# A gated delta rule with its slots refilled: four banks for the output transposes, first gathers first, no zero products, and two of four gate products in slots 10 and 11

## Chip, core and metric

The kernel runs on one core of one Trainium2 chip. The metric is device time in microseconds (us) of one execution. Engines are named as in the profile: PE (TensorE matmuls), PEld (its weight loads), DVE (VectorE), ACT (ScalarE), POOL (GpSimd), SP (SyncE).

## The reference, cut to what matters

Two layers, post-normed, on x of 16 sequences of 512 tokens with 256 channels, all in float32: gated linear attention, a mixture of 8 experts (top 2), the gated delta rule, and an MLP whose weights are composed from 32 of 64 primitives.

```python
x = _layernorm(x + _L0_attn_ref(x, ...))       # gated linear attention
x = _layernorm(x + _L0_ffn_ref(x, ...))        # mixture of experts
x = _layernorm(x + _L1_attn_ref(x, ...))       # gated delta rule, below
x = _layernorm(x + _L1_ffn_ref(x, ...))        # MLP with composed weights
# _L1_attn_ref: H = 4 heads, keys of 64, values of 128
h = rmsnorm(layernorm(x)); q, k, v = silu(causal_conv4(h @ Wq / Wk / Wv)); q, k = l2norm(q), l2norm(k)
g = -exp(A_log) * softplus(h @ Wa + dt_bias); beta = sigmoid(h @ Wb)
S = S * exp(g_t); S = S + k_t (x) ((v_t - k_t S) * beta_t); o_t = q_t S           # over 512 tokens
o = rmsnorm(o) * silu(h @ Wg); x = x + o @ Wo; out = gelu(layernorm(x) @ W2 + b2) + x
```

## The kernel before

The program is a sequence of stages, each with a queue written by hand for every engine and semaphores between them: `linear_attention`, `route` (router's top 2, slot tables and, beside them, the composed weights), `experts_mlp`, `delta_rule`, `mlp`. Engines meet in a barrier between stages.

`route` sums 16 pairs of weight tiles (`compose1`, `compose2`) into four PSUM banks `acc`. `edge(first)` (L248 on) multiplies a tile of zeros into all four banks, to open the sums with `start=True` and again to close them. It is called four times; `acc_done` behind the closing ones lets ScalarE copy the banks out.

`delta_rule` handles one sequence b (512 tokens, four chunks of 128) as a pipeline over periods. In period b four things run at once, told apart by flags: `ln`, the combination of expert outputs and the norms of sequence b+2; `front`, projections, convolutions and transposes to tokens of b+1; `here`, the inversion and the first two chunks of b; `past`, the last two chunks, gate, output norm, output projection and the dense layer of b-1; `end`, the last sum and norm of b-2. A loop runs the periods in pairs; the first and last ones stand outside it.

A period has 16 slots, two passes (pairs of chunks) of eight. In every engine's queue the order inside a slot is written out in its `period` function:

- PE. Slot n below 8: `project(n)`, with `to_tokens(n-2)` before it. `chunk(t, part)` in the slots of `CHUNK_AT`. Slots 0 and 8: `key_products`. Slots 5 to 7 and 13 to 15: three levels of the inversion (`first_half`, `second_half`), each of two tiles, which share the bank `UT` for T's transposes and have a bank each, `YZ[0]` and `YZ[1]`, for products. Slots 1 to 4: `gate(0..3)`, the products h @ Wg of b-1, all four through the bank `SIDE`. Slots 9 to 11: the four transposes `turn_o` of the gated output, through `SIDE` as well, each waiting for the copy of the one before (`turned_o` on ACT). Slots 11, 12: `mix_out`, o @ Wo, through `SIDE`.
- ACT. Slots 1 to 4: SiLU of the gate products. Slot 5: `squares(3)` and `squares_qk`, ahead of slot 6's copies `half_level`. Slot 8: `unit_o`, 16 scalings of the output, with one signal (`og`) at its end. Slots 9 to 11: `turned_o` and `rates`; slot 12: `rates(1)`, `channels(0)`.
- DVE. `products` turns the key products into nAT and QD, tile by tile; `conv(n-1)` in slot n; `last_sum(b-2)` and `last_norm(b-2)` in slots 9 and 10; `norm2(b+2)` in 10; `residual` in 11 and 12.
- SP and POOL. After `products` (semaphore `qd`) SP sends the 16x16 diagonal blocks of nAT to DRAM and gathers them for POOL, which inverts them (`invert_blocks`, 30 small instructions), and SP returns them into T (`return_blocks`). `first_half` of the lowest level (slots 5 and 13) waits for their landing (`t_in`). POOL also computes the powers -1/2 for all norms, gathers the expert rows (`gather_rows`, eight indirect DMAs a sequence) and, at the start of the stage, makes the constants (`ready`) before the first gather.

`mlp` (the last stage) copies the first block of its input behind the last (`tail_in`) and waits for that copy before it loads its weights.

## Time and profile before

| | |
|---|---|
| median of 3 runs | 4717.77 us (4705.86 to 4723.58) |
| profiled execution, its own time | 4709.05 us |
| its span, first to last instruction | 4707.4 us |
| granted TensorE clock, mean | 0.907 |
| busy: PE, PEld, DVE, ACT, POOL | 86%, 67%, 53%, 42%, 22% |
| instructions | 72598 |

The profile names each instruction by its line and tiles and says what ended the idle time before it. The granted clock is 1 at 2.4 GHz and 0.5 at 1.2 GHz; a mean over a stretch tells how much of it was at which level. A matmul of float32 shows as several records.

### The profile page before, as it was taken

The page shows a single profiled execution, that of the slowest core. Times are in us where ns is not written, and L with a number is a line of the kernel's source. Part 1 is how long each engine was busy: PE and PEld are TensorE (multiplying, and loading weights), DVE is VectorE, ACT ScalarE, POOL GpSimd, SP SyncE. Part 2 cuts the span into 40 slices and gives each one's busy share as a digit, 9 for nine tenths or more (in the row PEclk, how much of TensorE's full clock was granted, in tenths as well). Part 3 has the DMA queues.
Part 4 walks back from the last instruction along what each step waited for, and adds up shares of the span by engine and source line. Part 5 has one row for each costly group of instructions (what it writes and reads, how often), then busy time and mean ns, then how long its engine had stood idle before and what let it go on. Part 6 is the DMA issues. An engine that isn't in the chain of part 4 may idle for free. (4 is left out here: it accounts for less than half of the span.)

```text
span 4707.4 us, 72598 instructions
## 1 busy us (share of the span) xinstructions
PE 4038.7 (86%) x23892; PEld 3132.2 (67%) x23892; DVE 2471.9 (53%) x5457; ACT 1984.9 (42%) x4069; POOL 1055.9 (22%) x1689
## 2 busy tenths in 40 slices
PE   5887887689999999966888888888888888859998
PEld 3555555368888888854666667666666666646666
DVE  7888887432222222225666676766666766421111
ACT  5656564112112211214565565555555555422222
POOL 0111111101221122123333333333333332200000
PEclk8888888899999999987899898888898988879999
DMA  1100100344555555541111111111111110011111
GB/s 33 37 32 27 41 28 28 102 139 171 179 181 189 185 179 181 190 131 52 37 37 37 42 37 41 41 41 32 40 33 37 41 40 21 22 37 58 58 57 46
DMA packets 220431, 345.98 MB, mean 73 GB/s; under 512 B 99956, under 2 KB 171380, under 8 KB 201972
## 3 DMA queue, kind: packets, MB, share of 16 engines
q1 hardware_dynamic: 196404, 271.69, 18.2%
q0 software_dynamic: 23760, 71.07, 4.8%
q8 instruction: 126, 2.06, 0.2%
q14 instruction: 141, 1.16, 0.1%
HBM read 275.56 MB, written 67.63 MB: 73 GB/s over the span
## 5 line engine op out<-in xcount | busy, mean ns | idle before, releaser
L539 ACT ACTIVATE moe_rel<-moe_fc 128x512 f32<-128x512 f32 x284 | 169.6, 597 | 798.7 <-PE moe_fc L504 798.7
L504 PE MATMUL moe_fc<-moe_xT,moe_win 128*128 128x256 f32 x2272 | 504.0, 380 | 1.5 <-issue 0.8
L515 PE MATMUL moe_o<-moe_wout,moe_hT 128*128 128x256 f32 x2272 | 502.0, 379 | 0.0
L504 PEld LDWEIGHTS moe_fc<-moe_xT,moe_win 128*128 128x128 f32 x2272 | 432.9, 191 | 61.2 <-issue 2.1
L515 PEld LDWEIGHTS moe_o<-moe_wout,moe_hT 128*128 128x128 f32 x2272 | 426.3, 190 | 55.1
L563 DVE TENSOR_TENSOR moe_hT<-moe_rel 128x512 f32<-128x512 f32 x284 | 196.6, 692 | 366.5 <-ACT moe_rel L539 366.5
L1781 DVE SCALAR_TENSOR_TENSOR gdr_y<-gdr_bank,gdr_cw,gdr_y 128x511 f32<-128x511 f32 (+2 forms) x384 | 287.5, 749 | 52.6 <-ACT gdr_y L2045 29.0
L2242 PE MATMUL gdr_bank<-gdr_hT,gdr_wqkv 128*128 128x512 f32 x512 | 282.5, 680 | 21.3 <-ACT gdr_qk L2060 15.8
L572 DVE COPY moe_osb<-moe_o 128x512 f32<-128x512 f32 x71 | 49.1, 692 | 424.9 <-PE moe_o L515 424.9
L2361 PE MATMUL gdr_bank<-gdr_ident,gdr_T 128*128 128x128 f32 x768 | 132.5, 301 | 126.5 <-DMA gdr_T<-blocks_in 76.0
L693 PE MATMUL ffn_fc<-ffn_xT,ffn_win 128*128 128x512 f32 x512 | 224.0, 596 | 2.0 <-DMA ffn_win<-ffn_w 2.0
L704 PE MATMUL ffn_o<-ffn_wout,ffn_hT 128*128 128x256 f32 x1024 | 225.2, 381 | 0.0
L737 DVE TENSOR_TENSOR ffn_z<-ffn_o,ffn_xres 128x512 f32<-128x512 f32 x32 | 20.6, 686 | 384.3 <-PE ffn_o L704 384.3
L2365 PE MATMUL gdr_bank<-gdr_T,gdr_nAT 128*128 128x64 f32 x1536 | 215.6, 289 | 0.0
L718 ACT ACTIVATE ffn_hT<-ffn_fc 128x512 f32<-128x512 f32 x128 | 76.4, 597 | 328.2 <-PE ffn_fc L693 328.2
L2361 PEld LDWEIGHTS gdr_bank<-gdr_ident,gdr_T 128*128 128x128 f32 x768 | 102.6, 157 | 166.8 <-issue 74.6
L704 PEld LDWEIGHTS ffn_o<-ffn_wout,ffn_hT 128*128 128x128 f32 x1024 | 193.2, 190 | 27.6
L2365 PEld LDWEIGHTS gdr_bank<-gdr_T,gdr_nAT 128*128 128x128 f32 x1536 | 211.6, 213 | 0.0
L1673 POOL TENSOR_TENSOR gdr_rstd<-gdr_var,gdr_mhalf 128x4 f32<-128x4 f32 x64 | 65.1, 1017 | 648.7 <-DVE gdr_var L91 500.7
L2142 ACT COPY gdr_U<-gdr_bank 128x512 f32<-128x512 f32 x192 | 112.4, 585 | 215.2 <-PE gdr_bank L2361 206.1
L2242 PEld LDWEIGHTS gdr_bank<-gdr_hT,gdr_wqkv 128*128 128x128 f32 x512 | 100.3, 212 | 138.3 <-issue 84.0
L693 PEld LDWEIGHTS ffn_fc<-ffn_xT,ffn_win 128*128 128x128 f32 x512 | 97.8, 191 | 118.9 <-issue 118.2
(394 smaller groups left out, 8591.8 us busy)
## 6 DMA issues: line engine op xcount, KB each, us to landing
moe_win<-in_moe_w SPq DMA_DIRECT2D x71, 1024.0 KB, 8.0
moe_wout<-in_moe_w SPq DMA_DIRECT2D x71, 1024.0 KB, 5.1
slots_out<-moe_osb POOLq DMA_DIRECT2D x71, 256.0 KB, 7.4
ffn_xin<-mixed_rows SPq DMA_DIRECT2D x17, 512.0 KB, 3.8
gla_xp<-in_xT_rows SPq DMA_DIRECT2D x16, 512.0 KB, 4.7
gla_xres<-in_x_rows SPq DMA_DIRECT2D x16, 512.0 KB, 3.9
token_rows<-gla_x POOLq DMA_DIRECT2D x16, 512.0 KB, 3.4
rt_W<-in_fc_b SPq DMA_DIRECT2D x32, 256.0 KB, 3.3
```

The costliest lines, as they stand in the source:

```text
L504: ins = nc.tensor.matmul(fc_ps[j][:, m % 2, :], win[u][:, c, m * P:(m + 1) * P], xT[:, c, :], start=(c == 0), stop=(c == DT - 1))
L515: ins = nc.tensor.matmul(o_ps[u][:, t, :], hT[u][:, k, t * P:(t + 1) * P], wout[u][:, k, :], start=(k == 0), stop=(k == FT - 1))
L539: nc.scalar.activation(rel[:, j, :, :], fc_ps[j][:], ACT.Relu).then_inc(relu_done, 1)
L563: nc.vector.tensor_tensor(hT[u][:, 2 * j:2 * j + 2, :], rel[:, j, :, :], rel[:, j, :, :], ALU.mult).then_inc(h_ready, 1)
L693: ins = nc.tensor.matmul(fc_ps[m % 4][:], win[:, c, m * P:(m + 1) * P], xT[:, c, :], start=(c == 0), stop=(c == DT - 1))
L704: ins = nc.tensor.matmul(o_ps[t // 2][:, t % 2, :], hT[:, k, t * P:(t + 1) * P], wout[:, k, :], start=(k == 0), stop=(k == FT - 1))
L718: nc.scalar.activation(hT[:, m, :], fc_ps[m % 4][:], ACT.Gelu_apprx_tanh).then_inc(h_ready, 1)
L1781: ins = stt(y[:, n % 4, d:L], bank[FRONT[n % 2]][:, 0:L - d], cw[:, n, 3 - d:4 - d], y[:, n % 4, d:L], ALU.mult, ALU.add)
L2142: done("U", n, copy(U[t][:], heads(bank[UT][:])))
L2242: ins = mm(bank[FRONT[n % 2]][:], wqkv[:, c, n * P:(n + 1) * P], hT[:, c, :], start=(c == 0), stop=(c == DT - 1))
L2361: ins = tp(bank[UT][:, h * P:(h + 1) * P], T[:, i, h, :], ident[:])
L2365: ins = mm(bank[YZ[i]][:, h * HP:(h + 1) * HP].rearrange("p (m n) -> p m n", n=half), nAT[:, i, h, :], first, start=True, stop=True)
```

## The change

It changes which slot holds what, and the banks; the computation is the same. In words:

1. `route`: the products with zeros are gone. The first real product opens each sum and the last closes it; ScalarE waits for `used` in place of `acc_done`.
2. `mlp`: the tail copy is issued behind the weights, and waited for there.
3. Delta rule, start: the first input load is SP's first transfer; the gathers of sequence 0 are POOL's first work, the gathers of sequence 1 follow in its period -2, and the constants come behind them. PE, DVE and ACT wait for `ready` at the start of period -1 and not of the stage; DVE scales the weights in slot 5 of period -2.
4. `products`: all nAT of a pair first, with a semaphore `na` of their own that SP's `send_blocks` waits for, then all QD.
5. `gate(2)` and `gate(3)` of b-1 stay, now in slots 1 and 2; `gate(0)` and `gate(1)` of sequence b itself are made in slots 10 and 11 of period b, in the banks `YZ`, with their SiLUs in ACT's slot 12. PE waits for those (and for the second residual) before slot 13's first half.
6. `turn_o(0..3)` in slot 9, one bank each (`UT`, `YZ[0]`, `YZ[1]`, `SIDE`), each waiting only for its head's scaling; `unit_o` by heads in slots 7 and 8; `mix_out(0)` at the start of slot 10 in `SIDE`, `mix_out(1)` in slot 11 in `UT`.
7. ACT: `squares(3)` and `squares_qk` in slot 6 behind the level's copies, `decay_keys(2)` and `(3)` in slot 11, `lengths_u` in slot 12. PE: `rates` ahead of `to_tokens(7)` in slot 9. DVE: `last_sum` in slot 2, `last_norm` in 4, `lengths` in 7, `rates` in 9 and 10, `residual` in 10 and 11, `norm2` in 11, `rms` in 13 and 14. POOL: the power for `last_norm` ahead of the others.

```diff
@@ route @@
-                def edge(first):
-                    for bank in acc:
-                        ins = mm(bank[:], zero[:, 0:P], zero[:], start=first, stop=not first, skip_group_check=True)
-                    return ins
-                                 start=False, stop=False, skip_group_check=True)
+                                 start=(k == 0), stop=(k == KT - 1), skip_group_check=True)
-                    act.wait_ge(acc_done, n + 1)
+                    act.wait_ge(used, DEEP + KT)
@@ mlp, sync @@
-                sp.dma_start(x_rows[bass.ds(n_blocks * BLK, BLK), :], x_rows[0:BLK, :]).then_inc(tail_in, 16)
                 sp.dma_start(xin[:], rows(0)).then_inc(x_in, 16)
-                sp.wait_ge(tail_in, 16)
...
                     sp.dma_start(wout[:], v_src).then_inc(wout_in, 16)
+                    sp.dma_start(x_rows[bass.ds(n_blocks * BLK, BLK), :], x_rows[0:BLK, :]).then_inc(tail_in, 16)
+                    sp.wait_ge(tail_in, 16)
@@ delta_rule @@
+        TURN_O, MIX, GATE = (UT, YZ[0], YZ[1], SIDE), (SIDE, UT), (YZ[0], YZ[1], SIDE, SIDE)
@@ sync @@
-                    sp.wait_ge(s["qd"], b * TT + 2 * pair + 2)
+                    sp.wait_ge(s["na"], b * TT + 2 * pair + 2)
@@ gpsimd @@
+                gather_rows(0)
+                identity_tile(nc, pool, ident, id0, id1)
...
+                    if not later(b, -2):
+                        pool.wait_ge(got_used, 1)
+                        gather_rows(1)
+                        constants()
@@ vector, products @@
-                    for t in (2 * pair, 2 * pair + 1):
-                        i = t % 2
-                        wait("kk", t + 1)
+                    for i in range(2):
+                        wait("kk", 2 * pair + i + 1)
                         for k in range(2):
-                            stt(nAT[:, i, k::2, :], made[:, 0, :, :], -1.0, DT_[i][:, k::2, :], ALU.mult, ALU.mult)
-                            ins = tt(QD[t][:, k::2, :], made[:, 1, :, :], DT_[i][:, k::2, :], ALU.mult)
+                            ins = stt(nAT[:, i, k::2, :], made(i, k)[:, 0, :, :], -1.0, DT_[i][:, k::2, :], ALU.mult, ALU.mult)
+                        done("na", 2 * pair + i + 1, ins)
+                    for i in range(2):
+                        t = 2 * pair + i
+                        for k in range(2):
+                            ins = tt(QD[t][:, k::2, :], made(i, k)[:, 1, :, :], DT_[i][:, k::2, :], ALU.mult)
                         done("qd", t + 1, ins)
@@ vector, period @@
+                        if slot == 2 and end:
+                            last_sum(b - 2)
+                        if slot == 4 and end:
+                            last_norm(b - 2)
-                        if slot == 9 and end:
-                            last_sum(b - 2)
-                        if slot == 10 and end:
-                            last_norm(b - 2)
@@ scalar, period @@
+                        if past and slot == 9:
+                            turned_o(0, b - 1)
+                            turned_o(1, b - 1)
                         if front and 2 <= slot <= NP_ + 1:
                             spread_out(slot - 2, b + 1)
+                        if past and slot == 9:
+                            turned_o(2, b - 1)
+                            turned_o(3, b - 1)
+                        if past and slot == 8:
+                            unit_o(2, b - 1)
+                            unit_o(3, b - 1)
-                        if past and 1 <= slot <= TT:
-                            gate(slot - 1, b - 1)
+                        if past and 1 <= slot <= 2:
+                            gate(slot + 1, b - 1)
+                        if past and slot == 6:
+                            squares(3, b - 1)
+                        if front and slot == 6:
+                            squares_qk(b + 1)
+                        if past and slot == 7:
+                            unit_o(0, b - 1)
...
+                        if here and slot == 12:
+                            gate(0, b)
+                            gate(1, b)
@@ tensor @@
-                    wait("oTe", c) if c else wait("og", 1)
+                    wait("og", c + 1)
+                        if past and slot == 10:
+                            mix_out(0, b - 1)
                         if here and lv >= BASE:
+                            if slot == 13 and past:
+                                pe.wait_ge(s["xe"], b * 2)
+                            if slot == 13:
+                                pe.wait_ge(s["gt"], b * TT + 2)
                             first_half(lv, 2 * pair, b)
...
+                        if here and slot in (10, 11):
+                            gate(slot - 10, b)
+                        if past and slot == 11:
+                            mix_out(1, b - 1)
```

## Rows read from the trace of the kernel before

**Rows 1.** Delta rule's stage, busy time (PE, PEld, DVE, ACT, POOL, clock, GB/s)

```profile
2079.00:4222.00 2143.00, 1737.95 (x10688) 1380.06 (x10688) 1371.30 (x3170) 1169.83 (x2787) 683.84 (x1280) 0.87 0.14 37
```

**Rows 2.** Waits, TensorE, twelve periods from 2423.6 to 3919.0: us, times, longest

```profile
PE gdr_bank L2361 <- ACT gdr_U L2142: 41.3, 12, 3.4
PE gdr_bank L2361 <- DMA gdr_T<-blocks_in: 37.5, 12, 4.4
PE gdr_bank L2249 <- ACT gdr_y L2050: 36.0, 12, 3.0
PE gdr_bank L2386 <- ACT gdr_o L2102: 27.1, 12, 2.7
PE gdr_bank L2386 <- ACT gdr_y L2149: 23.5, 24, 1.2
```

**Rows 3.** Busy time in three stretches of one steady period

```profile
3043.00:3076.00 33.00, 27.18 (x131) 15.86 (x130) 23.36 (x53) 22.05 (x48) 9.35 (x31) 0.99 0.17 44
3076.00:3110.00 34.00, 30.56 (x177) 25.32 (x177) 20.06 (x38) 13.95 (x29) 10.27 (x4) 0.76 0.08 29
3110.00:3145.00 35.00, 26.43 (x160) 22.47 (x160) 26.59 (x68) 23.29 (x68) 12.43 (x31) 0.80 0.10 23
```

**Rows 4.** Timeline, TensorE: start, length, line, tiles, count [idle before]

```profile
3070.20 1.98 PE L2242 MATMUL gdr_bank<-gdr_hT,gdr_wqkv 128*128 128x512 f32 x4 [0.28 <-ACT gdr_qk L2060]
3075.91 1.11 PE L2361 MATMUL gdr_bank<-gdr_ident,gdr_T 128*128 128x128 f32 x4 [3.73 <-DMA gdr_T<-blocks_in]
...
3091.84 0.79 PE L2361 MATMUL gdr_bank<-gdr_ident,gdr_T 128*128 128x128 f32 x4 [3.44 <-ACT gdr_U L2142]
...
3098.18 3.73 PE L2242 MATMUL gdr_bank<-gdr_hT,gdr_wqkv 128*128 128x512 f32 x4
```

**Rows 5.** Timeline, SyncE's transfers of the first pair's blocks

```profile
3049.29 3.64 SPq L1575 DMA_DIRECT2D blocks_out<-gdr_nAT  x8
...
3069.74 4.58 SPq L1587 DMA_DIRECT2D gdr_T<-blocks_in  x8
```

**Rows 6.** Groups, VectorE, twelve periods: busy, mean ns | idle before

```profile
L1862 DVE TENSOR_TENSOR gdr_QD<-gdr_bank,gdr_DT 128x256 f32<-128x256 f32 x96 | 39.8, 415 | 0.0
...
L97 DVE TENSOR_SCALAR gdr_x<-gdr_n,gdr_agg,gdr_rstd 128x256 f32<-128x256 f32 x48 | 26.5, 611 | 1.0
...
L1940 DVE TENSOR_TENSOR gdr_n<-gdr_x,gdr_xa 128x1024 f32<-128x1024 f32 x12 | 14.7, 1226 | 0.4
```

**Rows 7.** Timeline, ScalarE, slots 5 and 6

```profile
3087.88 0.31 ACT L2118 ACTIVATE gdr_scr<-gdr_o 128x128 f32<-128x128 f32 x1
...
3089.19 1.91 ACT L2093 ACTIVATE gdr_sq<-gdr_qk 128x2048 f32<-128x2048 f32 x1
```

**Rows 8.** Timeline, ScalarE, unit_o of the last batch

```profile
4171.59 4.78 ACT L2102 ACTIVATE gdr_o<-gdr_o,gdr_orr 128x128 f32<-128x128 f32 x16 [4.41 <-POOL gdr_orr L1673]
```

**Rows 9.** Groups, ScalarE, twelve periods

```profile
L2112 ACT ACTIVATE gdr_gt<-gdr_bank 128x512 f32<-128x512 f32 x48 | 28.7, 597 | 10.4 <-PE gdr_bank L2287 9.5
...
L2112 ACT ACT_TABLE_LOAD x12 | 15.4, 1283 | 7.3 <-PE gdr_bank L2287 6.7
```

**Rows 10.** Timeline, TensorE, first mix_out of the last batch

```profile
4183.81 5.73 PE L2394 MATMUL gdr_bank<-gdr_wo,gdr_y 128*128 128x256 f32 x16 [0.73 <-ACT gdr_y L2149]
```

**Rows 11.** Busy time: the constants' stretch, and the second gathers' stretch

```profile
2080.86:2085.94 5.08, 0.00 (x0) 0.00 (x0) 0.00 (x0) 0.00 (x0) 4.28 (x14) 0.50 0.88 244
2117.68:2127.50 9.82, 8.04 (x16) 3.72 (x15) 1.78 (x3) 2.06 (x3) 7.68 (x8) 0.56 0.60 199
```

**Rows 12.** Timeline, TensorE, first projection

```profile
2120.98 2.93 PE L2242 MATMUL gdr_bank<-gdr_hT,gdr_wqkv 128*128 128x512 f32 x3 [1.56 <-ACT gdr_hT L2040]
```

**Rows 13.** Groups, TensorE, route stage (862 to 1048)

```profile
L251 PE MATMUL rt_acc<-rt_zero 128*128 128x512 f32 x32 | 14.4, 592 | 0.0
```

**Rows 14.** Timeline, SyncE, head of the last MLP

```profile
4225.63 0.62 SPq L620 DMA_DIRECT2D mixed_rows<-mixed_rows  x1
...
4230.61 0.36 SPq L628 DMA_DIRECT2D ffn_win<-ffn_w  x1
```

More of the change, by code:

```diff
@@ L224, in _ @@
                 act.wait_ge(w_col, 2)
-                for n, landed, scaled in ((0, in1, scaled1), (1, in2, scaled2)):
+                for n, landed, scaled, used in ((0, in1, scaled1, used1), (1, in2, scaled2, used2)):
                     for k in range(KT):
@@ L1974, in period @@
                             reset(b)
+                        if slot == 2 and end:
+                            last_sum(b - 2)
                         if slot == 3 and ln:
                             mix(0, b + 2)
+                        if slot == 5 and not later(b, -2):
+                            weights_ready()
                         if slot == 4 and past:
@@ L2148, in turned_o @@
                     wait("oT", c + 1)
-                    done("oTe", c + 1, copy(y[:, c, :], bank[SIDE][:]))
+                    done("oTe", c + 1, copy(y[:, c, :], bank[TURN_O[c]][:]))
                 def turned_n(c, b):
@@ L2162, in period @@
                     w = 1 - u
+                    if isinstance(b, int) and b == -1:
+                        act.wait_ge(ready, 1)
                     for slot in range(2 * (LEVELS + 1)):
@@ L2199, in period @@
                             decay_keys(slot - 1, b)
[L2200 to L2207 removed]
+                        if here and slot == 11:
+                            decay_keys(2, b)
+                            decay_keys(3, b)
                         if front and slot == 12:
@@ L2213, in period @@
                             keep_keys(b + 1)
+                        if ln and slot == 12:
+                            lengths_u(b + 2)
                         if past and slot == 14:
@@ L2450, in period @@
                             first_half(lv, 2 * pair + 1, b)
+                        if front and slot == 9:
+                            rates(b + 1)
+                        if past and slot == 9:
+                            if here:
+                                pe.wait_ge(s["qd"], b * TT + TT)
+                            turn_o(0, b - 1)
+                            turn_o(1, b - 1)
                         if front and 2 <= slot <= NP_ + 1:
@@ L2455, in period @@
                             second_half(lv, 2 * pair + 1, b)
-                        if past and 1 <= slot <= TT:
+                        if past and 1 <= slot <= 2:
                             if slot == 1 and here:
```

187 lines of the change are left out of this document (81 added, 106 removed).

## The prediction, before the result was known

> **What bounds the kernel now.** I read the stages first. Between 2079 and 4222 us lies the delta rule, 2143 us of the 4707, with TensorE busiest (1738), and almost all of the diff is in it; the route stage and the last MLP get one small edit each [rows 1]. Then the waits of TensorE over twelve steady periods, 2423.6 to 3919.0 us, so 124.6 us a period. The reader is to see that few causes make the idle time; the five largest are 165.4 us, 13.8 a period: the first half of level 5 waiting for a copy of U by ScalarE (41.3), level 4 waiting for the inverted blocks to come back by DMA (37.5), the last turn to tokens waiting for its SiLU (36.0), the output transposes waiting for their scaled input (27.1) and for the one bank they share (23.5) [rows 2]. Third, the granted clock in one period, which begins at about 3043: 0.99, 0.76 and 0.80 in its first three stretches [rows 3]. A wait is therefore paid twice. Before the 3.44 us wait at 3091.84 four projection matmuls took 1.98 us, after it the same four took 3.73 [rows 4]: the engine had gone from the 2.4 GHz level to the 1.2 GHz level. From 3091.84 to 3101.91, the end of that row, work is done that takes a little over half as long at the higher level: I take 4.8 us as the price of one drop in a busy stretch (an estimate from the doubled rows).
>
> **The change part by part.** I followed each queue in its new order by hand through the period that begins at 3043, with the durations of the rows; times are on that period's clock.
>
> *Block transfers.* The chain that ends the DMA wait begins with the last QD product, then come eight sends from 3049.29, the block load, the inversion on POOL, the return, eight scatters from 3069.74, and slot 5 at 3075.91 [rows 4, 5]. The sends now wait for the second tile's nAT only, and the QD products come behind. Each tile has two nAT and two QD products of equal shape, and 96 QD products of 415 ns are in these periods [rows 6]. Three or four of them leave the chain, and they overlap a little; I take 1.3 us (0.8 to 1.7). Removing gate products from slots 3 and 4 gains nothing here: TensorE gets to slot 5 earlier and waits longer. Slot 5 starts 1.3 us earlier.
>
> *last_sum and last_norm move to slots 2 and 4 of VectorE.* That is 1.23 us for the sum, about 2 for statistics and variance (an estimate: eight small instructions behind it) and 4 x 0.61 for the scaling [rows 6], ahead of R and of two convolutions. R is 1.3 us later, convolution 2 as well, then project(4) ends at about 3073.3, before the blocks land at 3074.6. The DMA chain covers it; without that cover it would cost up to 5.6 us.
>
> *squares(3) and squares_qk move from slot 5 to slot 6 of ScalarE, behind both tiles' U and Y copies.* They begin at 3087.88, take 1.28 and 1.91 us [rows 7] and stood between the end of first_half(5,0) and the copy that frees the bank. With them gone the copy ends about 1.4 us after the transposes begin, and TensorE waits some 0.3 us and not 3.44. The drop behind it has no cause left, so 4.8 us goes too. What is late next is tap(6), by 1.5 us, hidden behind spread_rates in slot 7. Today slots 5 to 7 take 34.1 us, to 3110.0 (the second stretch of rows 3). Less 3.1 of wait, less 4.8 of clock, and with 0.6 of small waits put back, it is 26.8: slot 8 starts at 3074.6 + 26.8 = 3101.4, 8.6 us earlier.
>
> *Output transposes.* unit_o (16 instructions, 4.78 us [rows 8]) goes to slots 7 and 8, its four heads signal separately, and the four transposes have a bank each, so the waits of 27.1 and 23.5 us over twelve periods (4.2 a period) go [rows 2]. The 3.0 us wait for SiLU(7) shrinks to about 0.5, because rates and two transposes are now ahead of it. In exchange mix_out(0) waits: ScalarE's queue has SiLU(7) to 3109.1, QSe (1.1), two copies, a spread copy and two copies (0.6 each) ahead of it, so it starts at 3113.3, and TensorE is ready at about 3110.8. A new wait of 2.4 us or a little more.
>
> *Two gate products come into slots 10 and 11.* Each is of the shape of a projection, 1.98 us at the higher clock and 0.1 less when the next one follows at once [rows 4]: 3.8 us, here on TensorE's path. Their SiLUs stand in slot 12 of ScalarE behind QSe, squares(0), two exponentials and three XT copies, and need a table load of 1283 ns that is new, because the exponentials come before them; then 2 x 0.60 [rows 9]. first_half(4,2) waits for them. The sum of slots 8 to 12: TensorE is busy 26.4 us there today [rows 3], of which I put 4.1 to the lower clock (the doubled transposes and chunk products behind 3122); with 3.8 for the gates that is 26.1 us of work. Up to the end of chunk(1,0) it is 24.0 (reach and channels come later), with waits of 0.5 and 2.5: 3128.4. ScalarE then has QSe 1.1, squares 1.3, exponentials 0.4, XT copies 2.2 with their matmuls, table 1.3, SiLUs 1.2: 7.5 us, to 3135.9. TensorE is free at 3132.6 (2.1 of work, 2.1 of short waits for ScalarE). A new wait of 3.3 us, with slot 13 and everything behind it queued. The second pair's blocks, a chain of 29 us today from QD to landing, begun at 3104.8 on nAT, have landed by 3134. Slot 13 starts at 3136.0 where it started at 3145.2: 9.2 us earlier, if the clock stays at its higher level.
>
> *The table load* shows 1.28 us here, with the activation 0.01 us behind it. The Trainium skill (ScalarE: Activation LUTs, What ACT_TABLE_LOAD costs) puts a switch at 1283 ns plus a drain of 1380. By the page the new wait would be 4.7 us and the gain 7.8; the row decides, 9.2.
>
> *Clock.* The new wait of 3.3 us, behind three short ones in slot 12, is as long as the one at 3091.84 that led to a drop. I take one new drop at slot 13, up to 4.8 us and by my count 4.5, since part of it falls on waits. Of the wait of 2.4 us before mix_out(0) I assume that the clock bears it; B is the other case. So a steady period gains 9.2 - 4.5 = 4.7 us. Bounds: 9.2 with no drop, 0.2 with two. Fourteen periods (1 to 14) give 66 us.
>
> *Period 0 and 15* are held at slots 5 and 13 by the block transfers; they gain 1.3 twice, and period 0 also its smaller U wait and the drop: 5 and 3 us (bounds 2 to 8 and 0 to 5).
>
> *Tail.* In the last batch unit_o starts at 4171.59 and mix_out at 4183.81, 12.2 us later [rows 8, 10]. With unit_o and the transposes overlapped it is 4.8, one transpose and one copy, 6.8 us; with the second mix_out no longer waiting for the first residual, 6.5 us of gain (4 to 9).
>
> *Start of the stage.* The first gathers start some 5.8 us earlier (the constants, 5.1 us, and the identity are no longer ahead), and so does all up to the first transposes. But the constants now stand behind gather_rows(1) on POOL, whose eight gathers take 9.8 us and begin at 2117.68 today [rows 11], so at 2111.9: 2111.9 + 9.8 + 5.1 = 2126.8. `ready` comes then, period -1 of TensorE, VectorE and ScalarE waits for it, and TensorE's first projection is at 2120.98 today [rows 12]. That is 5.8 us later; taking the rates ahead of to_tokens(7) in that period returns 2.5. Net +3.4 us (-6 to +7).
>
> *Route.* 32 records of products with zeros, 14.4 us, with no idle time before them [rows 13]. By my count the place of the first group is partly taken by a wait for the weight tiles (1 us), that of the third by VectorE's work between the two halves of the spots (1.2 us), and the groups overlap their neighbours a little: I take 11.6 us (8 to 14).
>
> *Last MLP.* The weights are issued at 4230.61, when the tail copy issued at 4225.63 has landed [rows 14]; now some 4.3 us earlier. The input transfer, transposes and copies stay ahead of the first product: 2 us of gain (0 to 4.3).
>
> Sum: -66 - 5 - 3 - 6.5 + 3.4 - 11.6 - 2 = -90.7, of which 25 outside the steady periods. The profiled execution took 4709.05 us (span 4707.4 and 1.65 around it), which gives 4618. It was 8.7 below the median of the runs, 4717.8, so I forecast 4627 against that median.
>
> **The rivals.** (A) No new drop: the waits are less long than I count, or fall so that the clock stays up. 9.2 a period: 129 + 25 = 154 us, about 4564. For it: the first stretch keeps a clock of 0.99 though TensorE is busy 27 of 33 us in it [rows 3]. (B) Two drops a period, at mix_out(0) and slot 13: the steady periods gain 3 us together, and with the 25 outside them it is about 4690. For it: the clock of 0.80 in the same slots now, where waits of 1 to 3 us come in a row. The Trainium skill (TensorE: Matmul & The Clock Gate, Part 1) says the engine's default is the throttled level and only sustained activity releases it; that speaks for B, and the rows of 0.76 and 0.80 agree [rows 3]. (C) VectorE becomes the bound: last_sum and last_norm ahead of the convolutions are not covered by the transfers. 5.6 us a period back: +0.9 a period, 13 - 25, about 4706. Against it: VectorE is busy 23 of 33 us there [rows 3]. (D) Slower: the clock stays at 1.2 GHz from slot 9 to slot 13. About 26 us of TensorE's work lies there; 16 us more than at the higher level, less the 9.2, is +6.8 a period: 95 - 25, about 4788. It decides once the lower level costs more than 9.2 + 25/14 = 11 us a period. Against it: the four transposes now run without waits between them.
>
> **How the numbers follow.** Chances: forecast 0.40, A 0.20, B 0.19, C 0.10, D 0.11. This kernel's measurement tells 0.5% (24 us) from no change. Forecast, A, a little over half of B and a small part of C are under 4694: faster 0.72; the rest of B and C, 0.17, within; D slower, 0.11. Range 4562 to 4700: A is its low end, B lies inside its high one, C and D are left out.
>
> **What would show it.** Right: periods of about 120 us; L2361's wait for U near nothing; the wait for blocks shorter than or like 3 us at slot 5; a new wait of about 3 us at slot 13 with a SiLU as its releaser, and a lower clock behind it; TensorE's first projection some 6 us later in its stage; L251 gone and the route stage about 12 us shorter. Wrong: periods of 124 us or more, VectorE work (L1940) as releaser of R's wait and longer, or a wait of over 5 us before mix_out.

## The result, and the profile after

The changed kernel took 4675.7 us (median of 6 runs, 4655.5 to 4684.8) where the kernel before took 4711.8 (6 runs): a ratio of 0.992, 95% interval 0.989 to 0.994, so 36 us or 0.8% faster. I had forecast 91 us. The profiled execution took 4669.46 us, with a span of 4667.5.

Waits of TensorE after, over the same twelve periods as [rows 2], now 2416.5 to 3895.2 us (us, times, longest):

```profile
PE gdr_bank L2254 <- ACT gdr_qk L2059: 52.2, 24, 2.7
PE gdr_bank L2373 <- issue: 40.7, 12, 3.4
PE gdr_bank L2261 <- ACT gdr_y L2049: 27.4, 19, 2.1
PE gdr_bank L2289 <- ACT gdr_gam L2072: 26.9, 12, 2.2
PE gdr_bank L2318 <- DVE gdr_R L1886: 24.3, 12, 2.4
PE gdr_bank L2406 <- ACT gdr_y L2147: 18.0, 12, 2.2
PE gdr_bank L2373 <- DVE gdr_T L1874: 9.8, 9, 2.2
PE gdr_bank L2373 <- DMA gdr_T<-blocks_in: 6.7, 9, 1.4
```

The wait for U (41.3 in [rows 2]) has shrunk to 0.3 a period, that for the blocks from 37.5 to 6.7, those of the output transposes are gone. In their place stand a wait for the spread copies in slots 3 and 4 (52.2), the 3.4 us at slot 13 (40.7) and 1.5 us before mix_out (18.0). TensorE's idle time is 18.1 us a period before and 18.6 after: the waits have moved, not gone. What the period gained is in the busy time, 106.5 and then 104.6 us for the same products.

Four halves of periods of the kernel before, then four of the one after, from key products to key products (busy time of PE, PEld, DVE, ACT, POOL, then clock, DMA share, GB/s):

```profile
2923.30:2984.20 60.90, 52.85 (x299) 37.06 (x298) 42.77 (x90) 35.10 (x75) 19.35 (x34) 0.92 0.11 30
2984.20:3045.00 60.80, 52.74 (x373) 46.98 (x372) 42.96 (x109) 38.41 (x100) 23.27 (x45) 0.89 0.16 45
3045.00:3110.00 65.00, 55.74 (x298) 39.68 (x297) 42.73 (x90) 34.53 (x74) 19.61 (x34) 0.87 0.12 33
3110.00:3172.60 62.60, 52.69 (x375) 46.71 (x374) 42.85 (x108) 37.76 (x99) 23.47 (x45) 0.89 0.18 49
```

```profile
2912.50:2968.00 55.50, 44.92 (x266) 31.26 (x265) 44.50 (x103) 34.26 (x74) 16.94 (x34) 0.97 0.09 25
2968.00:3035.20 67.20, 57.48 (x374) 50.09 (x372) 40.08 (x95) 39.25 (x98) 27.73 (x45) 0.85 0.14 40
3035.20:3089.80 54.60, 45.33 (x291) 32.02 (x290) 44.51 (x102) 34.71 (x77) 16.89 (x34) 1.00 0.14 40
3089.80:3157.50 67.70, 57.25 (x382) 49.36 (x382) 40.57 (x96) 38.80 (x98) 27.50 (x45) 0.87 0.16 45
```

Two things are to be seen. The first half (slots 0 to 7) is faster, the second (slots 8 to 15) slower: in the mean of twelve periods 63.4 became 55.2, and 61.2 became 68.0. In the second half, the part up to slot 13's first transposes grew from 34.7 to 38.7 us, the rest from 26.5 to 29.3. And before there are two kinds of period: one of about 121.7 us with a clock of 0.92 in its first half, and one of about 127.6 with 0.87, nearly in turn (two of the twelve lie between; mean 124.6). After, all are alike, 122 to 125 (mean 123.2). I had worked through the long kind.

TensorE in slots 9 to 13 of one period after:

```profile
3099.17 1.11 PE L2261 MATMUL gdr_bank<-gdr_ident,gdr_y 128*128 128x128 f32 x4 [2.08 <-ACT gdr_y L2049]
3100.07 1.92 PE L2398 MATMUL gdr_bank<-gdr_ident,gdr_o 128*128 128x128 f32 x8
3103.42 6.10 PE L2406 MATMUL gdr_bank<-gdr_wo,gdr_y 128*128 128x256 f32 x16 [1.43 <-ACT gdr_y L2147]
...
3115.37 3.62 PE L2406 MATMUL gdr_bank<-gdr_wo,gdr_y 128*128 128x256 f32 x16
...
3128.54 1.11 PE L2373 MATMUL gdr_bank<-gdr_ident,gdr_T 128*128 128x128 f32 x4 [3.41 <-issue]
3129.45 1.81 PE L2377 MATMUL gdr_bank<-gdr_T,gdr_nAT 128*128 128x64 f32 x8
3131.05 1.65 PE L2318 MATMUL gdr_bank<-gdr_R,gdr_U 128*128 128x128 f32 x8
3132.53 0.60 PE L2373 MATMUL gdr_bank<-gdr_ident,gdr_T 128*128 128x128 f32 x4
```

The sixteen products of mix_out take 6.10 us at 3103.42 and 3.62 at 3115.37, and four transposes of T 1.11 us at 3128.54 and 0.60 at 3132.53. The same period in stretches, before (first two lines: up to slot 13's first transposes, then to the end) and after (the same two parts, then the 10.2 us from 3098.0):

```profile
3110.00:3145.20 35.20, 26.64 (x161) 22.67 (x161) 26.80 (x69) 23.49 (x68) 12.43 (x31) 0.81 0.10 23
3145.20:3172.60 27.40, 26.06 (x216) 24.04 (x214) 16.06 (x40) 14.27 (x32) 11.04 (x14) 1.00 0.28 83
```

```profile
3089.80:3128.50 38.70, 29.47 (x168) 23.57 (x168) 25.27 (x63) 24.00 (x61) 17.28 (x32) 0.83 0.09 21
3128.50:3157.50 29.00, 27.79 (x214) 25.80 (x214) 15.30 (x33) 14.80 (x38) 10.22 (x13) 0.94 0.26 77
3098.00:3108.20 10.20, 7.60 (x23) 6.25 (x24) 5.55 (x16) 7.91 (x15) 5.95 (x16) 0.50 0.20 61
```

The 1.2 GHz level sets in at 3098.0, inside the 2.08 us wait and before the wait for mix_out, and holds for 10.2 us (0.50 throughout). The level was there in these slots before the change as well (0.81); new is the one at slot 13, where the rest of the period ran at 1.00 and now runs at 0.94. The releaser that the profile gives for the wait at slot 13, "issue", names nothing; the real one is the SiLU, as ScalarE's timeline shows:

```profile
3125.83 1.28 ACT L2110 ACT_TABLE_LOAD   x1
3127.12 1.23 ACT L2110 ACTIVATE gdr_gt<-gdr_bank 128x512 f32<-128x512 f32 x2
```

It ends at 3128.35, TensorE starts at 3128.54. Outside the steady periods: the route stage is 166.4 us and not 178.1, and no product with zeros is in it. The start of the stage became 5.8 us longer (from the end of the experts to the first key products: 111.4, then 117.2):

```profile
2115.75 2.08 PE L2254 MATMUL gdr_bank<-gdr_hT,gdr_wqkv 128*128 128x512 f32 x2 [13.24 <-POOL gdr_id L1659]
```

The first projection itself is 7.1 us later in its stage (47.1 us behind the end of the experts, then 54.2), and 1.4 of that is made good by the first key products. Period 0 is 1.8 us shorter, period 1 is 1.2 longer, period 14 7.9 shorter, period 15 and the tail 7.5, the last MLP 0.8.

### The profile page after: what moved, and what is told of

Same layout as the page of the kernel before. It is cut to its first block and busy times, and to the rows that moved or that the text cites. A ratio compares the mean times of both kernels' runs of the same rounds, so it can differ in the third digit from the quotient of the medians.

```text
span 4667.5 us, 72640 instructions
## 1 busy us (share of the span) xinstructions
PE 4000.8 (86%) x23860; PEld 3103.2 (66%) x23860; DVE 2462.3 (53%) x5456; ACT 2008.2 (43%) x4083; POOL 1084.2 (23%) x1689
## 5 line engine op out<-in xcount | busy, mean ns | idle before, releaser
L690 PEld LDWEIGHTS ffn_o<-ffn_wout,ffn_hT 128*128 128x128 f32 x1024 | 193.4, 190 | 27.4
L2140 ACT COPY gdr_U<-gdr_bank 128x512 f32<-128x512 f32 x192 | 112.4, 585 | 137.3 <-PE gdr_bank L2373 127.8
```

Of the source, the lines that this page charges most:

```text
L690: ins = nc.tensor.matmul(o_ps[t // 2][:, t % 2, :], hT[:, k, t * P:(t + 1) * P], wout[:, k, :], start=(k == 0), stop=(k == FT - 1))
L2140: done("U", n, copy(U[t][:], heads(bank[UT][:])))
```

## The experiments

Halves and periods are means over periods 2 to 13, from the starts of the key products of slots 0 and 8, in the one execution of each run that was profiled. In e5 and e15 that was the slowest of five, 28 and 19 us above the median, so their typical periods are shorter than the table's; b1 is one execution. The chips fall into two groups: on group I the kernel before takes 4712 and 4718 us, on group II 4794 to 4800. Each experiment is compared with the kernel before on its own chip; e1 to e4 share a chip, so do a1, b1, e5 and e6, then e7 to e10, e11 to e14, and e15 and e16.

| run | group | us | ratio to before, 95% | period | halves |
|---|---|---|---|---|---|
| changed, first comparison | I | 4675.7 | 0.992 (0.989 to 0.994) | 123.2 | 55.2 + 68.0 |
| a1_changed | II | 4699.0 | 0.979 (0.976 to 0.982) | 124.5 | 55.8 + 68.7 |
| b1_before | II | 4790.0 | | 130.8 | 63.6 + 67.2 |
| e1_gates_back | II | 4606.3 | 0.960 (0.958 to 0.962) | 118.7 | 57.3 + 61.4 |
| e2_only_gates | II | 4896.4 | 1.022 (1.020 to 1.023) | 137.3 | 62.5 + 74.8 |
| e3_mix_later | II | 4663.4 | 0.973 (0.972 to 0.975) | 122.0 | 56.1 + 65.9 |
| e4_silu_early | II | 4643.3 | 0.969 (0.967 to 0.970) | 120.9 | 55.9 + 65.0 |
| e5_both | II | 4623.3 | 0.964 (0.962 to 0.966) | 121.1 | 58.1 + 63.0 |
| e6_lengths_later | II | 4675.1 | 0.976 (0.973 to 0.978) | 122.5 | 56.2 + 66.4 |
| e7_all_three | II | 4687.5 | 0.978 (0.975 to 0.981) | 123.4 | 55.9 + 67.5 |
| e8_back_lengths | II | 4713.3 | 0.983 (0.980 to 0.986) | 124.6 | 55.6 + 69.0 |
| e9_constants_first | II | 4685.4 | 0.977 (0.974 to 0.980) | 125.2 | 55.6 + 69.7 |
| e10_sums_back | II | 4660.5 | 0.971 (0.968 to 0.974) | 122.0 | 53.1 + 68.9 |
| e11_gathers_late | I | 4763.7 | 1.011 (1.008 to 1.014) | 128.3 | 67.1 + 61.2 |
| e12_back_sums_constants | I | 4595.7 | 0.975 (0.972 to 0.978) | 118.4 | 52.6 + 65.8 |
| e13_mix_silu | I | 4605.4 | 0.977 (0.975 to 0.979) | 118.2 | 55.6 + 62.6 |
| e14_kept_best | I | 4601.2 | 0.977 (0.974 to 0.980) | 118.7 | 52.7 + 66.0 |
| e15_kept_constants | II | 4624.7 | 0.964 (0.962 to 0.965) | 122.5 | 56.0 + 66.5 |
| e16_back_constants | II | 4594.0 | 0.959 (0.956 to 0.961) | 118.2 | 56.6 + 61.7 |

**The gate part undone, and alone.** In e1, TensorE's code, cut (ScalarE's likewise, and one bank for all four gates):

```
-                            if slot == 13:
-                                pe.wait_ge(s["gt"], b * TT + 2)
...
-                        if past and 1 <= slot <= 2:
+                        if past and 1 <= slot <= TT:
...
-                            gate(slot + 1, b - 1)
-                        if here and slot in (10, 11):
-                            gate(slot - 10, b)
+                            gate(slot - 1, b - 1)
```

> The changed kernel with all four gate products and their SiLUs back in slots 1 to 4 (one bank, one after the other), and no wait for gate outputs ahead of slot 13; the rest of the change stays. A mean period of the changed kernel is 123.2 us, 55.2 from slot 0 to slot 8 and 68.0 from slot 8 to the next slot 0. Theory 1 (moving the gates is paid back in the second half: the same 3.4 us of products, 2.1 us of low clock at slot 13 and its 3.4 us wait): second half falls by 6 to 8, first half rises by 4 to 7, the period is 121 to 123 and the kernel 0 to 30 us faster than the changed one. Rival (the gate part carries the gain, the rest of the change little): the period goes back to 125 or more, the kernel is 25 us or more slower than the changed one. My forecast's own terms would give a second half of about 61.5 and a period near 123.

Measured against a1, same group: first half +1.5, second half -7.3, the kernel 2.0% (93 us) faster, three times what Theory 1 allowed. The second half lies where Theory 1 had it; the first pays back less than the products it takes in (3.7 us), because they fill waits of slots 3 and 4: the wait for the spread copies is 16.0 us over the twelve periods and not 45.8. e2 is the reverse on the kernel before.

> The kernel before with the gate part alone: two gate products in slots 10 and 11 into the banks of the doubling steps, their SiLUs in slot 12, and the wait for them ahead of slot 13. Before: period 124.6, halves 63.4 and 61.2. Theory 1 (paid back): first half about 58 (3.3 of products and 2 of clock), second half about 67 (3.4 of products, 2.1 of clock at slot 13, 1 of waits), period 124 to 126, the kernel within 15 us of before. Rival (the gates fill waits that slots 9 to 12 had anyway, and the first half gains all of its 8): second half 64 or less and a period of 121 or less, 50 us faster than before.

Measured: first half 62.5 against 63.6 in b1, second half 74.8 against 67.2, 2.2% slower. Theory 1 had 5 us of gain in the first half and 6 of loss in the second; it was 1.1 and 7.6, part of which is the late signals treated below. Waits of TensorE in e2:

```profile
PE gdr_bank L2365 <- ACT gdr_gt L2113: 41.8, 12, 3.6
PE gdr_bank L2365 <- ACT gdr_U L2143: 41.3, 12, 3.5
PE gdr_bank L2281 <- ACT gdr_XT L2082: 38.5, 23, 4.9
```

The 3.5 us at slot 13 belong to the gate part alone, and the wait for U isn't touched by it. The third row is the late signals'.

**The two waits of the second half, one by one.** e3 moves the first output product behind chunk 0's second part:

```
-                        if past and slot == 10:
-                            mix_out(0, b - 1)
                         if here and lv >= BASE:
...
+                        if past and slot == 10:
+                            mix_out(0, b - 1)
                         if here and slot in (10, 11):
                             gate(slot - 10, b)
```

> The changed kernel with the first half of the output product issued behind the second part of chunk 0 in slot 10, not ahead of it, so that the work of that chunk covers the wait for the copies of the transposed outputs. Theory 1 (the wait of 1.4 us there, behind one of 2.1 us, brings a clock drop that makes this product 6.1 us instead of 3.6): wait gone and the product at full clock, second half 64 to 65, period 3 to 3.5 less, kernel 40 to 50 us faster than the changed one. Rival (the clock falls there for the 2.1 us wait for the last transposed convolution, whatever is behind): only the 1.4 us go, the low clock falls on the chunk instead, 15 to 20 us faster. Third (VectorE or ScalarE has no slack behind it): no difference.

e4 moves the gate SiLUs on ScalarE:

```
                         if here and slot == 11:
                             decay_keys(2, b)
                             decay_keys(3, b)
+                            gate(0, b)
+                            gate(1, b)
...
-                        if here and slot == 12:
-                            gate(0, b)
-                            gate(1, b)
```

> The changed kernel with the two gate SiLUs at the end of ScalarE's slot 11, ahead of the rates and channel copies of slot 12, so that the gate outputs are there well before slot 13. Theory 1 (the SiLUs at the end of slot 12 are late, and their 3.4 us wait brings the second clock drop): wait at slot 13 under 1 us, no drop there, period 3 to 5 less, kernel 40 to 70 us faster than the changed one. Rival (ScalarE's whole list of slots 11 to 12 is what is late, with one more function table load in it): TensorE waits as long for the exponentials and channel copies of slot 12 instead, period within 1 us, kernel within 15 us.

e3: second half -2.8, 0.6% faster than a1; e4: second half -3.7, 1.1% faster. In e3 the wait for mix_out fell from 17.3 to 5.2 us in twelve periods and both mix_outs took 8.1 us a period, from 9.3; at the higher level they take 7.2. The level of 1.2 GHz did not go from slots 9 to 12, it got shorter (10.2 us a period in a1, 3.4 or 6.8 in e3), so Theory 1 held for the larger part and the rival, by which the 2.1 us wait brings it, for the rest. e4 lay inside Theory 1's numbers: slot 13's first transposes began 1.8 us earlier with no wait, and what stands behind them took 1.9 us less; a stretch of 3.4 us at the lower level was left. e13 has both, on group I, where it can be set beside the first comparison.

> The changed kernel, gates kept, with the output product behind the chunk in slot 10 and the gate SiLUs in ScalarE's slot 11, without the later lengths, which sent the block transfers of the second pair late (a 4 us wait for them at slot 13 in each run that had them). Alone: 122.0 and 120.9 of 124.5. Theory (the forecast's missing 3 us a period are these two waits and their clock): second half 62 to 63.5, period 118 to 119.5, kernel 75 to 100 us faster than the changed one. Rival (each wait removed brings the next): period 120 to 121.5, 45 to 65 us faster.

```profile
PE gdr_bank L2253 <- ACT gdr_qk L2059: 50.3, 24, 2.7
PE gdr_bank L2288 <- ACT gdr_gam L2072: 42.3, 12, 3.5
PE gdr_bank L2260 <- ACT gdr_y L2049: 26.7, 17, 2.1
...
PE gdr_bank L2405 <- ACT gdr_y L2147: 2.4, 5, 0.7
```

The theory's numbers for the period were met: 68.0 became 62.6, the period 118.2. The kernel is at 0.977 of before where the change alone gave 0.992, 1.5% or 70 us (75 to 100 were expected). The wait at slot 13 is gone and the one for mix_out nearly; the table load now delays the exponentials instead (26.9 became 42.3), 1.3 us a period.

**The wait for SiLU(7).** e6 moves `lengths(b + 1)` on VectorE from slot 7 to slot 8.

> The changed kernel with VectorE's step on the key and query lengths in slot 8, behind the products and the last convolution, where it was in slot 7 ahead of both. Theory 1 (the 2.1 us wait for the last transposed convolution comes from those 2.3 us on VectorE and starts the clock drop): that wait falls to 0 to 0.5 us, the drop comes later or not at all, period 2 to 4 less, kernel 30 to 55 us faster than the changed one. Rival (the unit scaling of queries and keys then comes late, and TensorE waits for the transposes of slot 12 instead): the period stays within 1 us or grows, kernel within 15 us.

The wait shrank (from 23.9 to 12.9 us in twelve periods), and the kernel is 0.4% faster, short of the theory. What took the gain is neither rival:

```profile
PE gdr_bank L2373 <- DMA gdr_T<-blocks_in: 50.9, 17, 5.3
```

GpSimd's queue has the power step of these lengths ahead of the inversion of the second pair's blocks; with the lengths late, slot 13 waits 4.1 us a period for the blocks.

> The changed kernel with the gates back in slots 1 to 4 and the first half of the output product behind chunk 0's second part in slot 10: the first and third experiments together. Theory 1 (two separate prices, one at slot 13, one at slot 10): the period falls below the 118.7 of the gates back alone, by 1.4 for the wait and up to 2.1 for the clock, so 115 to 117.5, the kernel 20 to 45 us faster than with the gates back alone. Rival (the low clock is given out again elsewhere as soon as one wait goes): within 10 us of it.

> The changed kernel, gates kept in slots 10 and 11, with three edits at once: output product behind the chunk in slot 10, gate SiLUs at the end of ScalarE's slot 11, lengths behind the last convolution. Alone, on chips of this kind, they took the period from 124.5 to 122.0, 120.9 and 122.5. Theory 1 (the forecast's missing 3 us a period are these waits and their two clock drops, each its own): the parts add to about 8 us, period 116 to 119, second half 60 to 63, kernel 90 to 120 us faster than the changed one. Rival (each wait removed lets the next one bring the same drop): period 119.5 to 121, kernel 50 to 75 us faster.

> The changed kernel with the gates back in slots 1 to 4 (which alone gave a period of 118.7 and a kernel of 4606 us) and the lengths behind the last convolution. If the wait for that convolution brings the one low-clock stretch that is left in slots 9 to 12: period 115 to 117, 25 to 50 us faster than the gates back alone. If the low clock comes anyway after 20 us of slots 8 and 9, as it did when the output product alone was moved (121.1): no gain or a loss of up to 20 us.

e7 and e8 contain e6's edit and wait 3.3 and 4.3 us a period for the blocks. e5 doesn't, yet it waits 2.1 for them and is 0.4% slower than e1: it comes to slot 13 so early that the chain of transfers bounds it (without its wait it would begin 29.8 us behind slot 8, where e1 begins at 32.4, and the blocks land at 30 to 34). So the prices of e1, e3, e4 and e6 don't add, and all three fell short even of their rivals: e5 is 0.4% slower than e1 (19 us; the rival had 10), e8 2.4% slower (the rival had 20 us), and e7 0.1% faster than a1 (the rival had 50 us).

**Start of the stage.** e9:

```
+                        constants()
                         pool.wait_ge(got_used, 1)
                         gather_rows(1)
-                        constants()
```

> The changed kernel with GpSimd's constants made ahead of the gathers of the second batch, not behind them; the gathers of the first batch stay first. After the change TensorE sits 13.2 us ahead of its first projection for the last of the constants, which lie behind 10.9 us of gathers. Theory (this is why the start of the stage became 5.8 us longer and not 3.4): that wait falls to 2 to 3 us, the stage's start is 9 to 11 us shorter, the kernel 10 us faster. Rival (the gathers of the second batch, 5 us later, make its norm late): 0 to 5 us.

```profile
2104.70 1.22 PE L2254 MATMUL gdr_bank<-gdr_hT,gdr_wqkv 128*128 128x512 f32 x1 [1.82 <-POOL gdr_id L1659]
```

The wait fell from 13.24 to 1.82 us, and the start of the stage is 107.1 us long where a1's is 118.7. The total is 0.2% under a1, which the intervals don't part.

**VectorE's sums.** e10 puts last_sum and last_norm back.

> The changed kernel with the last sum and last norm back in slots 9 and 10 of VectorE (and their power step of GpSimd back behind the others), where they were before the change. My rival C was that in slots 2 and 4 they sit ahead of the scaling that TensorE waits for. If so: the two waits of 2 to 2.7 us in slots 3 and 4 shrink, first half 53 or less, kernel 20 to 40 us faster. If the chain of block transfers hides them: first half within 0.5 us of 55.8; and the sums, now in slots 9 and 10 ahead of the transposes' SiLU and residual, make the second half 1 to 4 us longer, kernel 15 to 60 us slower than the changed one.

My rival C in part: the first half is 2.7 us shorter, the second 0.2 longer, the kernel 0.9% faster. The transfers don't hide the sums in slots 2 and 4. But where slot 13 comes early (e12, e14), they cost as much in slot 9:

> The changed kernel with three things undone or mended: the gates back in slots 1 to 4 (period 118.7 alone), the last sum and last norm back in slots 9 and 10 (122.0 alone, of 124.5), and the constants ahead of the second gathers (12 to 14 us alone). If the parts add: period 116 to 117, kernel 4555 to 4575 us on a chip where before takes 4795, a ratio of 0.952. If the first half, once the sums are away, meets the same wait for block transfers and the sums then lengthen slots 9 and 10: period 118 to 119, 4590 to 4600.

> The run above with the last sum and norm back in slots 9 and 10 and the constants ahead of the second gathers: the gates kept with all that was found to help. With the parts adding (2.5 a period and 10 us): period 116 to 117, kernel 4560 to 4580 us, level with the gates back. If moving gates into slots 10 and 11 is a loss whatever stands around it: 20 us or more slower than the gates back with the same two edits.

Both have first halves of 52.6 and 52.7 and second halves of 65.8 and 66.0. GpSimd in e12:

```profile
3061.48 1.01 POOL L1664 TENSOR_TENSOR gdr_rstd<-gdr_var,gdr_mhalf 128x4 f32<-128x4 f32 x1 [7.61 <-DVE gdr_var L91]
3062.46 0.84 POOL L1670 TENSOR_TENSOR gdr_vblk<-gdr_wblk,gdr_low 64x256 f32<-64x256 f32 x1
```

The inversion follows the last norm's power step without a pause, 8.6 us after GpSimd came free, where in e13 it waits 3.1 us for its own blocks: the second pair is held up for a sum it has nothing to do with, and TensorE waits 3.4 us (e12) and 1.9 us (e14) for it.

**Two groups of chips.**

> The changed kernel unaltered, on the chip of the other runs of this group, since the kernel before took 4795 us on the chip of the first four experiments and 4712 on that of the first comparison. If the chip shifts both kernels alike, the ratio to before is 0.99 again. If it shifts the kernel before alone (for one, by a DMA chain that this chip serves later), the ratio is near 0.975 on such a chip and all of the first experiments have to be read against that.

> The kernel before unaltered, for its profile on this chip. If the chip is like that of the first four experiments, its period is 3 to 6 us longer than the 124.6 of the first profile, and the longer part shows which wait moved; if it is like the first, 124.6 with halves of 63.4 and 61.2.

The same two kernels differ by 96 us on a chip of group II and by 36 on one of group I. The kernel before is 83 us slower there, 72 of them in twelve periods' second halves (67.2 against 61.2). Its ScalarE, TensorE and GpSimd in b1:

```profile
3068.90 0.78 ACT L2154 ACTIVATE gdr_h2T<-gdr_bank,gdr_bb,gdr_g 128x512 f32<-128x512 f32 x1 [3.26 <-remote]
3069.79 0.59 ACT L2142 COPY gdr_U<-gdr_bank 128x512 f32<-128x512 f32 x1
3071.84 0.37 ACT L2144 COPY gdr_Y<-gdr_bank 128x256 f32<-128x256 f32 x1 [1.47 <-remote]
```

```profile
3066.82 0.94 PE L2365 MATMUL gdr_bank<-gdr_T,gdr_nAT 128*128 128x64 f32 x7
3067.60 1.06 PE L2377 MATMUL gdr_bank<-gdr_Y,gdr_U 128*128 128x64 f32 x8
3072.36 1.94 PE L2377 MATMUL gdr_bank<-gdr_Y,gdr_U 128*128 128x64 f32 x8 [3.69 <-ACT gdr_Y L2144]
```

```profile
3060.16 1.09 POOL L1667 DMA_INDIRECT gdr_got<-slots_out,gdr_ix  x1 [0.84 <-POOL gdr_ix L1661]
...
3069.90 0.95 POOL L1667 DMA_INDIRECT gdr_got<-slots_out,gdr_ix  x1 [0.31 <-issue]
```

The copy of Y starts at 3071.84, 4.1 us after its product's end at 3067.76 and 1.0 us after GpSimd has issued the last of its eight gathers; "remote" means that no event in the trace released it. TensorE then waits and falls to the lower clock. In the profiles of group II the last such late start of most periods comes 11.3 to 12.5 us after the first gather's start; in those of group I there is none. In a1 they come 1.3 to 1.6 us behind the last gather's issue, and VectorE has them too. In the changed kernel ScalarE's are the copies of slot 15 (`turned`, L2039: 38.9 us in 11 times), and a1's second half is 0.7 us longer than on group I; in e2 they are the XT copies of slot 13 (51.9 us in 10). e11 holds the gathers back until the first key products:

> The kernel before, with GpSimd's eight gathers of a period held until TensorE has made that period's first key products; they ran in the last 12 us of the period before. On the second kind of chip (kernel before 4795 us) the copies that wait for TensorE in slots 14 and 15 begin 2.4 to 4 us after their products, and the last of them always 12.4 us after the first gather's start, in the changed kernel too; on the first chip nothing of the kind is seen. Theory (the gathers hold TensorE's signals up on such a chip): the late copies leave slots 14 and 15, second half 61 to 62 and not 67.2, the same delay shows up in slots 0 to 2 where it costs 0 to 4, period 125 to 128, kernel 40 to 90 us faster than before. Rival (the delay belongs to the code of slot 14 or to another transfer there): period within 1 us of 130.8.

It ran on group I, where there was no late start to move. There the later gathers cost 3.7 us of the first half (the blocks' inversion stands behind them on GpSimd, the wait for the blocks is 6.0 us a period, from 3.1) and the kernel is 1.1% slower. That the gathers cause the late starts is therefore argued from their timing, not shown.

**The gate part, last.**

> The changed kernel with the gates kept, the output product behind the chunk in slot 10, the gate SiLUs in ScalarE's slot 11 (together a ratio of 0.977 to before, a period of 118.2), and the constants ahead of the second gathers; the last sum and norm stay in slots 2 and 4, since back in slots 9 and 10 their power step held the second pair's blocks up. If the 9 us of the stage's start add: 4590 to 4600 where before takes 4718, ratio 0.973 to 0.976.

> The changed kernel with the gates back in slots 1 to 4 and the constants ahead of the second gathers, sums in slots 2 and 4. If the gates in slots 10 and 11 are worth nothing once their waits are gone: within 10 us of the run above. If gates in slots 1 to 4, with no function table load in slot 12 and no wait at slot 13, are better in themselves: 10 to 25 us faster than the run above, 4565 to 4585 where before takes 4718.

With each version's waits mended, the gates in slots 1 to 4 are the better on group II, 4594.0 against 4624.7. Part of that is the late starts, which in e15 fall on the U and Y copies of slot 15 in some periods (these last 126 to 130 us, the rest 118 to 121). In group I the pair that differs so is e12 and e14 (sums back in both): 4595.7 and 4601.2, no difference. Neither pair differs in the gates alone: e14 and e15 also have e3's and e4's edits. So with its waits mended the gate part is worth nothing on the one group and costs on the other. The gates back without the sums was not run on group I. e16 beats both kernels: 0.959 of before, and a1 on that group is at 0.979. On group I the best run was e12, 0.975.

## Why the prediction fell short

**Slots 0 to 7: the size right, by two misses that cancel.** Forecast 8.6 us earlier at slot 8, measured 8.2 in the mean. The sums in slots 2 and 4, which I took as covered by the transfers, were not: slot 5 begins 0.4 us earlier and not 1.3, and taking them out is worth 2.7 in this half (e10). Slots 5 to 7 gained more than I had, 7.8 for 7.3; the wait for U went from 3.4 to 0.3 us a period, as forecast.

**"So a steady period gains 9.2 - 4.5 = 4.7 us": the term that failed.** It measured 1.4 in the mean of twelve. Over its 14 periods the kernel gained 23 us and not 66, which is 43 of the 51 us that lie between the forecast's sum (90.7) and the two profiled executions (39.6). By parts of the period (us):

| part | that period: before, forecast, measured | mean of twelve: before, after | change forecast, change in the mean |
|---|---|---|---|
| slots 0 to 7 | 65.0, 56.4, 54.6 | 63.4, 55.2 | -8.6, -8.2 |
| slot 8 to slot 13's first transposes | 35.2, 34.6, 38.7 | 34.7, 38.7 | -0.6, +4.0 |
| from there to the next slot 0 | 27.4, 31.9, 29.0 | 26.5, 29.3 | +4.5, +2.8 |
| period | 127.6, 122.9, 122.3 | 124.6, 123.2 | -4.7, -1.4 |

- The failed step lies in slots 8 to 12, 4.6 us a period off. Their sum takes 4.1 us off TensorE's work, as if the 1.2 GHz level went from these slots, and holds that "of the wait of 2.4 us before mix_out(0) I assume that the clock bears it". It did not: of the 10.2 us from 3098.0 at that level TensorE is busy 7.60, which by half is 3.8 us lost (an estimate). The level sets in with the wait for SiLU(7), which I had put at 0.5 us and which is 2.1; the wait before mix_out is 1.4, where I had 2.4 to 2.5. These three come to 4.3 us too little, near the 4.1 by which that period's row is off. That is rival B's outcome, two drops a period, and B's time (4690) was nearer than my own, though B has the first drop at mix_out and it sets in one wait earlier. e3 prices the wait before mix_out with its share of the lower level at 2.8 us a period.
- The drop at slot 13 came, and I had it too large: what stands behind slot 13's start grew by 2.8 us and not 4.5.
- The base. I took the change from one period, 3045.0 to 3172.6, and multiplied by 14. Its total came out, 122.3 for 122.9, but that is luck: the three parts are off by -1.8, +4.1 and -2.9. And the mean before is 124.6, because nearly every other period is of about 121.7 us with a clock of 0.92 in its first half, so there was less clock to win in it. [rows 2] gave 124.6; I had the number and didn't ask why my period was 3 us longer. This is a second view of the same 3.3 us a period, not to be added to the first.

**The wait for the gate SiLUs at slot 13: right,** 3.3 forecast, 3.4 measured, with the drop behind it. Wait and drop were put at 7.8 together; e4, which takes both away, gains 3.7 us a period, since the exponentials then wait 1.3 longer. **The table load** is the row's 1.28 us with the activation 0.01 us behind it, here too, and the copy ahead of it ends 0.02 us before the load starts. The Trainium skill (ScalarE: Activation LUTs, What ACT_TABLE_LOAD costs) has a further 1380 ns of drain; that would have made the wait 4.7, and it was 3.4, so the trace doesn't agree. **The clock.** The lower level set in 0.9 us into a wait of 2.08 us, with no wait of TensorE in the 12 us ahead of it. The Trainium skill (TensorE: Matmul & The Clock Gate, Part 1) has the lower level as the default, which the row does not contradict.

**Route: right,** 11.6 forecast, 11.7 measured. **Start of the stage:** +3.4 forecast, +5.8 measured: the mechanism, constants behind the second gathers, was right (13.2 us of waiting). The first projection was 7.1 us later and not 5.8, and 1.4 us came back behind it and not 2.5. **Periods 0 and 15 with the tail:** -14.5 forecast, -9.3 measured, most of the miss in period 0 (-5, -1.8). **Last MLP:** -2, -0.8. **Rival C** was right that the transfers don't hide the sums, but not in its size. **Rival D** didn't happen. **Rival A**'s time (4564) no run reached, the nearest was 4594.

## What to carry to other kernels

Where periods are not alike, work a change through in one of each kind, and check that the base is the mean. A wait of TensorE was paid here in idle time and again in clock, so a change that took waits out of one half of the loop and put new ones into the other earned little: find for each new wait the work of the same engine that could stand ahead of it (e3 and e4, 1.5% together in e13). Take a stretch at the lower level off a sum only if all waits ahead of it are gone. Before moving a small step on one engine, look at what stands behind it in the other engines' queues: a power step in GpSimd's queue, ahead of the step that feeds a DMA chain, went with 2 to 4 us a period of waiting for the blocks in five runs that delayed it (e6, e7, e8, e12, e14); in e10 the wait for the SiLUs covered it.

## What the runs showed of the hardware

TensorE's granted clock fell to the 1.2 GHz level inside a wait of 2.08 us and stayed there for 10.2 us, of which the engine was busy 7.60 (3098.0 to 3108.2 after the change). Taking the next wait, of 1.4 us, mostly away left 3.4 or 6.8 us at that level (e3). A load of ScalarE's function table took 1.28 us, with no pause ahead of it or behind it.

One kernel took 4712 to 4718 us on two measurements and 4794 to 4800 us on four other chips, and the change between two kernels was 36 us on the one kind and 96 on the other. On the slower kind, copies that wait for TensorE start 2.4 to 4.1 us after its modelled end, during GpSimd's issue of eight indirect DMAs or 1.0 to 1.6 us behind the last of them. Why, and what sets the chips apart, stays open.
